# A fused Mamba-2 and mixture-of-experts block: the sum of squares of a tile taken by TensorE over eight channel blocks in place of GpSimd's tree of additions

## What is computed

```python
xn  = layernorm(x)                                  # 2048 x 512
z, xBC, dt = split(xn @ in_proj_w.T)                # 1024, 1280, 16 columns
x_, B, C = split(silu(conv4(xBC)))                  # 1024, 128, 128
y   = state_space_scan(x_, B, C, dt, A) + x_ * D_skip
y   = y * silu(z)                                   # 2048 x 1024
y   = y * rsqrt(mean(y * y, axis=-1) + 1e-5)        # over 1024 channels
out = x + (y * norm_w) @ out_proj_w.T + moe(xn)
```

## Time and profile before

| | |
|---|---|
| median of three runs | 809.78 us (805.66 to 812.03) |
| profiled execution, span from first to last instruction | 805.9 us |
| TensorE (PE) busy, whole span | 672.9 us, 84% |
| VectorE (DVE) busy | 536.0 us, 67% |
| ScalarE (ACT) busy | 374.9 us, 47% |
| GpSimd (POOL) busy | 335.3 us, 42% |
| mean granted TensorE clock, share of full speed | 0.917 |

### The profile page before, as it was taken

The page is one execution under the profiler, slowest core; times in us unless marked ns, Lnnn a source line. Parts: engine busy times, 40 slices in busy tenths (PEclk is TensorE's granted clock), DMA queues, the critical chain, the costliest instruction groups (busy, mean ns, idle before and its releaser), DMA issues.

```text
span 805.9 us, 13821 instructions
## 1 busy us (share of the span) xinstructions
PE 672.9 (84%) x4176; PEld 537.8 (67%) x4177; DVE 536.0 (67%) x1046; ACT 374.9 (47%) x768; POOL 335.3 (42%) x294
## 2 busy tenths in 40 slices
PE   1554439899999947679999999989999989999774
PEld 0232228899999937677776877867877777787442
DVE  5667663344444418958879688688788688788554
ACT  3333013344444425485665475465557357456410
POOL 4456013222222107224555646446465365555541
PEclk9766658999999977799999999999999999999898
DMA  8886114544444344232332522422432332243221
GB/s 271 264 282 244 52 20 152 175 127 116 127 125 130 118 155 177 101 92 80 105 92 93 156 67 80 146 66 79 142 114 69 105 122 61 78 130 105 68 54 49
DMA packets 32485, 96.43 MB, mean 120 GB/s; under 512 B 5120, under 2 KB 5888, under 8 KB 30016
## 3 DMA queue, kind: packets, MB, share of 16 engines
q1 hardware_dynamic: 24720, 67.96, 24.6%
q0 software_dynamic: 7728, 28.05, 12.8%
HBM read 73.06 MB, written 22.94 MB: 119 GB/s over the span
## 4 chain that ended last, share of the span: by engine, by line
PE 51%; issue 13%; DVE 13%; POOL 10%; DMA 8%; ACT 3%; SPq 0%; POOLq 0%; DVEq 0%; ACTq 0%
PE pi L1248 16%; PE pg L823 10%; PE pd L834 7%; PE po L1520 4%; PE py L1541 4%; DVE xs L1203 3%; PE py L1548 3%; DMA xn_d<-xin 2%; DMA xin<-in_x 2%; POOL y L1158 2%; PE px L810 2%; DVE y L1398 2%; POOL xdd L1132 2%; POOL ysq L1112 2%; PE pxb L1582 2%
## 5 line engine op out<-in xcount | busy, mean ns | idle before, releaser
L1203 DVE SCALAR_TENSOR_TENSOR xs<-raw,conv_w,xs 128x256 f32<-128x256 f32 x240 | 130.9, 616 | 3.4 <-ACT xs L1181 3.4
L1248 PE MATMUL pi<-xh,wh 128*128 128x256 f32 x576 | 101.4, 300 | 25.6 <-DVE wl L1021 10.8
L1520 PE MATMUL po<-wo,y 128*128 128x512 f32 x256 | 114.4, 600 | 1.1 <-POOL y L1161 0.7
L1248 PEld LDWEIGHTS pi<-xh,wh 128*128 128x128 f32 x576 | 82.0, 197 | 30.6 <-issue 24.5
L1248 PE MATMUL pi<-xh,wl 128*128 128x256 f32 x576 | 96.0, 290 | 0.0
L1248 PE MATMUL pi<-xl,wh 128*128 128x256 f32 x576 | 95.2, 288 | 0.0
L1520 PEld LDWEIGHTS po<-wo,y 128*128 128x128 f32 x256 | 48.2, 193 | 56.4 <-issue 55.2
L1248 PEld LDWEIGHTS pi<-xh,wl 128*128 128x128 f32 x576 | 82.6, 197 | 0.0
L1248 PEld LDWEIGHTS pi<-xl,wh 128*128 128x128 f32 x576 | 82.1, 196 | 0.0
L1282 ACT ACTIVATE m<-m,cst 128x128 f32<-128x128 f32 x256 | 79.4, 388 | 0.5
L1158 POOL TENSOR_TENSOR y<-y,e 128x1024 f32<-128x1024 f32 x15 | 35.8, 2388 | 65.2 <-DVE y L1398 65.2
(11 more groups left out here) (200 smaller groups left out, 1444.5 us busy)
## 6 DMA issues: line engine op xcount, KB each, us to landing
m<-cs_d SPq DMA_DIRECT2D x16, 1024.0 KB, 4.8
y_d<-yo SPq DMA_DIRECT2D x39, 256.0 KB
e<-cs_d SPq DMA_DIRECT2D x32, 256.0 KB, 4.2
gur<-in_w_gu POOLq DMA_DIRECT2D x8, 768.0 KB, 5.4
xin<-in_x SPq DMA_DIRECT2D x8, 512.0 KB, 4.8
xn_d<-xin SPq DMA_DIRECT2D x8, 512.0 KB, 4.9
xt_d<-xt SPq DMA_DIRECT2D x8, 512.0 KB, 3.7
xl<-xt_d SPq DMA_DIRECT2D x8, 512.0 KB, 3.7
```

Of the source, the lines that this page charges most:

```text
L1203: dve.scalar_tensor_tensor(out=xs[par][:, b, :], in0=raw[:, b, k:k + GT], scalar=conv_w[:, b, k:k + 1], in1=xs[par][:, b, :], op0=ALU.mult ...
L1248: mm = pe.matmul(pi[n % 2][:, h, :], ww[:, k, at:at + P], xx[:, k, :], start=k3 == 0, stop=k3 == 11)
L1520: mm = pe.matmul(po[:, :], y[:, b, :], wo[:, b, :], start=b == 0, stop=b == XB - 1)
```

## The change

The semaphore `tree`, the function `sums` and both of its calls are gone from GpSimd. TensorE waits for the squares themselves (`ysqd`) and multiplies each of the eight blocks of `ysq` with the column of ones, adding up in `pk[:, 2, 0:1]`.

```diff
-        tree = sem("tree")
...
         def gpsimd(pool):
...
-            pool.sem_inc(tree, 3)
...
-            def sums(t):
-
-                pool.wait_ge(ysqd, t + 1 + CR)
-                pool.tensor_tensor(ysq[:, 0:4, :], ysq[:, 0:4, :], ysq[:, 4:8, :], ALU.add).then_inc(tree, 1)
-                pool.wait_ge(tree, t * 3 + 4)
-                pool.tensor_tensor(ysq[:, 0:2, :], ysq[:, 0:2, :], ysq[:, 2:4, :], ALU.add).then_inc(tree, 1)
-                pool.wait_ge(tree, t * 3 + 5)
-                pool.tensor_tensor(ysq[:, 0:1, :], ysq[:, 0:1, :], ysq[:, 1:2, :], ALU.add).then_inc(tree, 1)
...
-                    if not first:
-                        sums(t - 1)
...
-            sums(T - 1)
             factor(T - 1)
...
                 mm.then_inc(op, 1)
-                pe.wait_ge(tree, t * 3 + 6)
+                pe.wait_ge(ysqd, t + 1 + CR)
                 if not static(t, T - 1):
                     pe.wait_ge(cbm_done, t + 2 + CR)
-                pe.matmul(pk[:, 2, 0:1], ysq[:, 0, :], ones[:, :], start=True, stop=True).then_inc(ss, 1)
+                for b in range(XB):
+                    mm = pe.matmul(pk[:, 2, 0:1], ysq[:, b, :], ones[:, :], start=b == 0, stop=b == XB - 1)
+                mm.then_inc(ss, 1)
```

## The result

The changed kernel takes 824.67 us (median of four runs, 822.06 to 827.01), the kernel before beside it on the same chip 810.49 us (four runs). The ratio is 1.0188, 95% interval 1.0144 to 1.0232: slower by 1.9%, +14.2 us. The forecast was +7.6 us, 817.4 us: the direction held, the size was half. The time lies above the forecast's own range of 814 to 822 us, and inside the wide one of 806 to 829 us only because that one takes in half of rival C.

The account below looks back on a forecast made before the run. TensorE was taken to set the pace in tiles 1 to 13; 10.4 - 2.5 - 0.3 = +7.6 us on the 809.78 us median gave 817.4 us. Its own range was 814 to 822 us, the wide one 806 to 829.

Parts of the forecast that it names:

- rival C: TensorE's burst of narrow products: the clock falls and slows `stage(2)` behind it, 1.5 us a tile; priced at 829 us, chance 0.18.
- 14 passes of 0.11 us a tile: TensorE, each tile: 16 narrow passes in place of two, 0.11 us for each further one, 1.54 us added.
- Waits for the tree and clock of `stage(2)`, tiles 6 and 10: TensorE: waits of 2.45 us (tile 6) and 2.35 (tile 10) go, and 2 x 1.5 us of low clock.
- VectorE 1.66 us a tile faster, worth nothing: VectorE's twelve taps without GpSimd's tree: 4.84 us in place of 6.50; worth nothing beyond tiles 6 and 10.
- Tiles 1 to 13: ... +10.4 us.: TensorE in tiles 1 to 13: 20.0 us of passes added, 6.6 us of waits and 3.0 of clock gone.
- loop turns of four tiles +1.7 us: Sign to check in TensorE's changed profile: each loop turn some 1.7 us longer, passes less the waits and clock regained.
- Tile 14 -2.5, tile 15 and the end -0.3: Tile 14: -1.3 us of gap, -1.2 of clock; tile 15 and end: -0.3 us, between +1.5 and -0.9.
- A: TensorE's narrow loads are pulled ahead under `po`, so the burst is free: -17 us, 793 us; chance 0.08.
- B: TensorE's narrow passes cost 0.05 us each, as 64-column loads do: -5.8 us, 804 us, no measurable change; chance 0.10.
- D: VectorE sets the pace, its 1.66 us a tile come through: at most 4.5 us of TensorE's waits, 813 us; chance 0.04.

Follow-up runs that it names:

- the passes alone: Kernel before, tree kept, with seven further narrow products of block 0 per tile into a column nobody reads: 839.61 us, ratio 1.0336.
- seven blocks: Changed kernel with seven narrow products a tile in place of eight, squares of channel block 7 left out: ratio 1.0128 to the kernel before.

## Why the prediction was right in direction and short by half

- *14 passes of 0.11 us a tile.* Right. The burst takes 1.70 us where I had 1.76. With TensorE's loop written out, the stretch of tiles 2 to 6 grew by 117.45 - 111.83 = 5.6 us and that of tiles 6 to 10 by 117.47 - 115.87 = 1.6 us. Forecast were 5.6 and 1.7, where the terms of the second add up to 1.6. The Trainium skill's two rules that I weighed differ here. "LDWEIGHTS (loading the stationary operand)" of "TensorE: Matmul & The Clock Gate", 107 ns a load, agrees with 1.70 us / 16 = 0.106 us. The 81 ns of its "Back-to-back issue gap", given there for pairs with 128 moving columns, are not reached by these pairs with one.
- *Waits for the tree and clock of `stage(2)`, tiles 6 and 10.* Right: the waits are gone, and `stage(2)` of tile 6 takes 2.88 us. VectorE's turn, which had made the tree late there, was not seen.
- *VectorE 1.66 us a tile faster, worth nothing.* Right on both: its twelve taps of tile 6 take 4.83 us (forecast 4.84), answering to the earlier trace rows, and between the projections of tiles 1 and 14 TensorE waits for VectorE no longer than before (`carry` 1.9, `zs` 1.7 us):

```profile
536.66 4.83 DVE L1189 SCALAR_TENSOR_TENSOR xs<-raw,conv_w,xs 128x256 f32<-128x256 f32 x12
...
544.32 0.69 DVE L1375 TENSOR_TENSOR e<-py,e 128x512 f32<-128x512 f32 x1 [0.84 <-PE py L1529]
```

  `decayed` now waits for TensorE, where I had expected TensorE to be close to waiting for it.
- *"Tiles 1 to 13: ... +10.4 us."* This is the step that failed. The sum priced the added passes by what they take on the array, and took it that TensorE goes from one turn of the loop into the next as before. That the body also has to stay loaded was no term of it. At 812 passes it no longer does, which costs 9.4 us in the profiled executions (7.9 us between the medians): 6.4 us of waits at the two turns, and most of the rest by the clock behind them. Without it my sum holds: the changed kernel with TensorE written out is 6.9 us over before, forecast +7.6. The check "loop turns of four tiles +1.7 us" was the one that showed it at once: +6.8 us.
- *Tile 14 -2.5, tile 15 and the end -0.3.* Mis-sized: -2.8 forecast, 56.53 - 58.37 = -1.8 us measured. The gap behind `po` shrank as forecast, but part of it went into a wait of `po` in tile 15 for GpSimd's `y` (1.45 us in place of 0.37), the next in line there.
- *Rivals.* A and B fall with the burst's 1.70 us. D falls with the run without the tree, where the waits for `zs` and `carry` stayed at 2.6 and 1.9 us. C said that the clock falls in the burst and slows `stage(2)` behind it; that takes 2.88 us, so it doesn't. The low clock was there behind another gap. That the wide range held is luck: it reached up to C's price (829), and C's mechanism was not the cause.

## What to carry to other kernels

Added instructions in a hardware loop have two prices, what they take on the engine and what they do to the length of the body. Read the profile page's instruction queues by engine and stretch. In these runs a body that stayed loaded had no packets from its first turn back on, and one that didn't had packets and an "issue" wait at its first instruction; there the loop written out gave back 7.9 us. And where a wait is found just behind a turn, look whether the engine that is waited for has an issue wait there itself, before the work that is late is made shorter: here both waits of the loop went without a change to the tree.

## What the runs showed of the hardware that I had not expected

- TensorE kept a body of 798 passes with their loads over the turns and did not keep one of 804; beyond the edge the two turns together cost 5.9 us of idle time at 804 passes and 6.4 at 812.
- Written out, the same code costs no wait, though it loads instructions all along (28 packets against 14).
- VectorE waited 7.6 us at the two turns already before (up to 3.9 each), and both waits went with its loop written out.
- A gap of 3.29 or 3.15 us had a clock of 0.57 or 0.50 behind it in the changed kernel, one of 3.01 us had 0.50 with the passes alone, and one of 3.15 us had 1.00 with seven blocks.
- VectorE's twelve taps took 6.50 us while GpSimd's additions ran and 4.83 us without them.
